# Context attentions of a small perceiver: transposes spread between products, rounding of the context moved to GpSimd

## The reference

```
q = xn @ Wq                      # 16 heads (32 wide or of other widths)
k, v = y @ Wk, y @ Wv            # y: the 1601 context rows of a batch, 128 wide
a = softmax(q k^T * scale)       # per batch and head: 64 x 1601
o = a v
```

## Time and profile before

| | |
|---|---|
| median of 3 runs | 2290.49 us (2285.55 to 2293.77) |
| the profiled execution | 2297.82 us |
| its span | 2296.0 us, 41893 instructions |
| TensorE busy | 2042.5 us, 89% |
| TensorE weight loads busy | 1749.3 us, 76% |
| VectorE busy | 1379.2 us, 60% |
| ScalarE busy | 1124.4 us, 49% |
| GpSimd busy | 512.6 us, 22% |
| granted TensorE clock, mean | 0.93 |

### The profile page before, as it was taken

One profiled execution on the slowest core, in us unless ns is written; L12 is line 12 of the kernel. 1 busy time (PEld: TensorE's weight loads), 2 busy tenths in 40 slices (PEclk: granted clock), 3 DMA queues, 4 the chain that ended last, 5 costly groups with the idle time before them and its releaser, 6 DMA issues. The chain is left out here.

```text
span 2296.0 us, 41893 instructions
## 1 busy us (share of the span) xinstructions
PE 2042.5 (89%) x14948; PEld 1749.3 (76%) x14948; DVE 1379.2 (60%) x2704; ACT 1124.4 (49%) x2256; POOL 512.6 (22%) x412
## 2 busy tenths in 40 slices
PE   4776999999886998489899999987979999999898
PEld 1654999999655885277699999956859999997577
DVE  6463777777445443831677777724447777776366
ACT  2243666666423432321566666613436666664254
POOL 2323222221011330200322222002332222220034
PEclk9687999999987998789999999977999999999799
DMA  5153010010041213432100100001221001000022
GB/s 211 25 233 128 31 45 31 29 44 0 26 156 57 79 53 136 188 139 83 45 30 31 45 29 29 0 13 66 78 83 45 31 30 44 29 15 0 19 78 76
DMA packets 32314, 144.01 MB, mean 63 GB/s; under 512 B 3632, under 2 KB 9136, under 8 KB 28848
## 3 DMA queue, kind: packets, MB, share of 16 engines
q1 hardware_dynamic: 32176, 142.23, 17.2%
HBM read 125.59 MB, written 13.90 MB: 61 GB/s over the span
## 5 line engine op out<-in xcount | busy, mean ns | idle before, releaser
L1037 ACT ACTIVATE pTh<-ps 128x512 fp32r<-128x512 f32 (+1 forms) x768 | 353.9, 519 | 382.5 <-PE ps L937 380.4
L1095 DVE TENSOR_TENSOR pTl<-ps,pTh 128x512 fp32r<-128x512 f32 (+1 forms) x768 | 415.7, 582 | 129.0 <-ACT pTh L1037 128.8
L637 PE MATMUL ps<-pTh,ch 128*128 128x256 f32 (+1 forms) x1248 | 383.5, 307 | 2.3 <-DVE pTl L1095 2.2
L638 PE MATMUL ps<-pTl,ch 128*128 128x256 f32 (+1 forms) x1248 | 348.4, 279 | 0.0
L639 PE MATMUL ps<-pTh,cl 128*128 128x256 f32 (+1 forms) x1248 | 348.0, 279 | 0.0
L637 PE MATMUL ps<-cTh,qh 128*128 128x512 f32 (+2 forms) x768 | 276.9, 361 | 15.2 <-POOL ql L891 8.0
L639 PE MATMUL ps<-cTh,ql 128*128 128x512 f32 (+2 forms) x768 | 269.6, 351 | 0.0
L638 PE MATMUL ps<-cTl,qh 128*128 128x512 f32 (+2 forms) x768 | 268.8, 350 | 0.0
L1082 DVE TENSOR_REDUCE top<-ps 128x1 f32<-128x802 f32 x192 | 189.2, 986 | 110.7 <-PE ps L639 110.7
L637 PEld LDWEIGHTS ps<-pTh,ch 128*128 128x128 f32 (+1 forms) x1248 | 235.1, 188 | 15.8 <-DVE pTl L1095 12.1
L638 PEld LDWEIGHTS ps<-pTl,ch 128*128 128x128 f32 (+1 forms) x1248 | 235.7, 189 | 0.0
(11 more groups left out here) (351 smaller groups left out, 3585.9 us busy)
## 6 DMA issues: line engine op xcount, KB each, us to landing
w<-l1f_w_in SPq DMA_DIRECT2D x16, 1024.0 KB, 8.0
raw<-ctxT_in SPq DMA_DIRECT2D x16, 801.0 KB, 4.3
raw<-ctx_in SPq DMA_DIRECT2D x14, 832.0 KB, 4.4
wg<-l0f_guide_in SPq DMA_DIRECT2D x10, 704.0 KB, 5.1
z<-ctx_in SPq DMA_DIRECT2D x8, 832.0 KB, 12.9
z<-z SPq DMA_DIRECT2D x8, 832.0 KB, 10.6
keys<-ctx_in SPq DMA_DIRECT2D x8, 832.0 KB, 11.2
zT<-zT SPq DMA_DIRECT2D x8, 801.0 KB, 14.0
```

The costliest lines, as they stand in the source:

```text
L637: pe.matmul(out, high, moving_high, start=start, stop=False)
L638: pe.matmul(out, high, moving_low, start=False, stop=False)
L1037: nc.scalar.activation(pTh[0:w, PARTS[g][0]:PARTS[g][0] + n, slot, :], ps[0:w, turned_bank[slot][g], 0:n * P].rearrange("p (k r) -> p k r" ...
L1095: dve.tensor_tensor(pTl[0:w, at, slot, :], ps[0:w, turned_bank[slot][g], 0:n * P].rearrange("p (k r) -> p k r", r=P), pTh[0:w, at, slot, : ...
```

## The change

Four edits in `cross_attention`:
- TensorE: `turn` issues one transpose. `scores` and `values` (now of one chunk) call a function after each product, which may issue one. Eight transposes of slot 1 stand between the score products of the first unit, five between the products of value chunks 0 to 2, and the thirteen of slot 0 in value chunks 5 to 12. The second unit's scores come behind value chunk 4, not 7.
- VectorE: the maximum of the first half is a function of its own and comes ahead of `low(0, v-1)`.
- ScalarE: `keep(2)` of slot 1 moves behind the exponentials of unit v; the second half of the exponential of unit v+1 moves behind `keep(2)` and `keep(3)` of slot 0. `high` is gone.
- GpSimd: `split` waits for `raw`, copies the leading part and subtracts, where `low` only subtracted.

```
@@ gpsimd
-                        def low(n, dst, high):
-
+                        def split(n, dst, high):
+
+                            pool.wait_ge(raw_landed, 16 * (n + 1))
+                            pool.sem_inc(raw_seen, 1)
+                            pool.tensor_copy(high, raw[:, 0:dst.shape[1]]).then_inc(high_ready, 1)
                             pool.wait_ge(high_ready, n + 1)
...
@@ tensor, scores
+                                cols = score_cols[n]
+                                pe.matmul(flat[:, cols], qh[:, k, at], cTh[:, i, cols], start=True, stop=False)
+                                beside(3 * n)
+                                pe.matmul(flat[:, cols], qh[:, k, at], cTl[:, i, cols], start=False, stop=False)
+                                beside(3 * n + 1)
+                                last = pe.matmul(flat[:, cols], ql[:, k, at], cTh[:, i, cols], start=False, stop=True)
                                 if n == 1:
                                     last.then_inc(scores_half, 1)
-                            last.then_inc(scores_ready, 1)
...
+                                if n == 3:
+                                    last.then_inc(scores_ready, 1)
+                                beside(3 * n + 2)
...
@@ tensor, body
-                                pe.wait_ge(probs_half, v)
-                                turn_second(0, v - 1)
-                                scores(u, step, first)
-                                turn_second(1, v - 1)
-                                turn_second(2, v - 1)
-                                values(0, c - 1, i, first and u == 2, new_batch)
-                                turn_second(3, v - 1)
-                                values(1, c - 1, i)
-                                scores(u + 1, step, first)
-                                turn_first(0, v)
-                                turn_first(1, v)
-                                values(2, c - 1, i)
-                                turn_first(2, v)
-                                values(3, c - 1, i)
-                                turn_first(3, v)
+
+                                def second_with_scores(n):
+                                    if 1 <= n < 5:
+                                        turn(0, n - 1, v - 1, 1)
+                                    elif n >= 8:
+                                        turn(1, n - 8, v - 1, 1)
+
+                                def second_with_values(n):
+                                    if n < 8 and n % 2 == 0:
+                                        turn(2, n // 2, v - 1, 1)
+                                    elif n == 8:
+                                        turn(3, 0, v - 1, 1)
+
+                                def first_with_values(n):
+                                    if 15 <= n < 19:
+                                        turn(0, n - 15, v, 0)
+                                    elif 19 <= n < 23:
+                                        turn(1, n - 19, v, 0)
+                                    elif 25 <= n < 33 and n % 2:
+                                        turn(2, (n - 25) // 2, v, 0)
+                                    elif n == 36:
+                                        turn(3, 0, v, 0)
+
+                                scores(u, step, first, second_with_scores)
+                                values(0, c - 1, i, second_with_values, first and u == 2, new_batch)
+                                for chunk in range(1, 4):
+                                    values(chunk, c - 1, i, second_with_values)
+                                values(4, c - 1, i)
+                                scores(u + 1, step, first, alone)
+                                for chunk in range(5, KCH):
+                                    values(chunk, c - 1, i, first_with_values)
...
@@ scalar, body
                                     keep(1, v - 1, 1)
-                                    keep(2, v - 1, 1)
                                 exponents(v, 0, first and u < 2, 0)
                                 exponents(v, 0, first and u < 2, 1)
                                 if before:
+                                    keep(2, v - 1, 1)
                                     keep(3, v - 1, 1)
-                                if at == 0 and not (final and i):
-                                    high(n, cTh[:, 1 - i])
-                                if at == 2 and not (final and i):
-                                    high(n + 1, ch[:, 1 - i])
                                 keep(0, v, 0, c if before else None)
                                 keep(1, v, 0, c if before else None)
                                 exponents(v + 1, 1, first and u < 2, 0)
-                                exponents(v + 1, 1, first and u < 2, 1)
                                 keep(2, v, 0, c if before else None)
                                 keep(3, v, 0, c if before else None)
...
+                                exponents(v + 1, 1, first and u < 2, 1)
...
@@ vector, body
+                                maximum_of_half(v, 0)
                                 if before:
                                     low(0, v - 1, 1)
                                 maximum(v, 0)
...
+                                maximum_of_half(v + 1, 1)
                                 maximum(v + 1, 1)
```

More of the change, by code:

```diff
@@ L914, in _, with scores @@
                     def _(pe):
-                        def scores(u, step, first):
+                        def scores(u, step, first, beside):
                             i = u // PER
@@ L933, in turn @@
[L933 to L945, removed]
-                                pe.wait_ge(low_kept, 4 * v)
-                            if g == 3:
-                                pe.wait_ge(low_kept, 4 * v + 1)
-                            turn(g, v, 0)
@@ L951, in turn_second, with turn @@
-                        def turn_second(g, v):
-                            pe.wait_ge(low_kept, 4 * v + (-2, -1, 0, 1)[g])
-                            turn(g, v, 1)
-                        def values(g, c, i, early=False, new_batch=None):
-                            if g == 0 and not early:
+                                if n == 3:
+                                    last.then_inc(scores_ready, 1)
+                                beside(3 * n + 2)
+                        def turn(g, k, v, slot, first=False):
+                            if k == 0 and slot:
+                                pe.wait_ge(low_kept, 4 * v + (-2, -1, 0, 1)[g])
+                            if k == 0 and not slot and g != 2 and (g == 3 or not first):
+                                pe.wait_ge(low_kept, 4 * v + (-1, 0, None, 1)[g])
+                            chunk = PARTS[g][k]
+                            w = keys_in(chunk)
+                            last = pe.transpose(ps[0:w, turned_bank[slot][g], k * P:(k + 1) * P],
+                                                probs[slot][:, chunk * P:chunk * P + w], ident[:])
+                            if chunk == PARTS[g][-1]:
+                                last.then_inc(turned_ready, 1)
@@ L959, in values @@
+                        def values(chunk, c, i, beside=None, early=False, new_batch=None):
+                            g = chunk // 4
+                            if chunk == 0 and not early:
                                 pe.wait_ge(value_kept, c)
@@ L979, in body @@
                                 if first and u == 0:
-                                    scores(u, step, first)
-                                    scores(u + 1, step, first)
+                                    scores(u, step, first, alone)
+                                    scores(u + 1, step, first, alone)
                                     for g in range(4):
-                                        turn_first(g, v, True)
+                                        for k in range(len(PARTS[g])):
+                                            turn(g, k, v, 0, True)
```

67 lines of the change are left out of this document (32 added, 35 removed).

## The result

The changed kernel is slower: 2334.47 us, median of 4 runs (2333.11 to 2336.07), against 2292.13 (4 runs) for the kernel before. The ratio is 1.0188, with a 95% interval of 1.0162 to 1.0214, so +42 us. The forecast was 2323.5, +33. Run again later, among the experiments, the same changed kernel took 2324.95 us (5 runs) against 2292.22: ratio 1.0155 (1.0131 to 1.0178), +33. Why the two differ is the first thing to settle, since the forecast was made on the attentions.

A forecast was written before the change was run, and what follows sets the result against it. TensorE's own instruction stream was taken as the bound. Couples +29.8 us and attention ends +3.1 gave +33, carried over to the shown median of 2290.49: 2323.5 us, range 2287 to 2342.

The forecast's parts named there:

- Transposes one by one: On TensorE, a single transpose costs 0.110 us between score products, 0.115 between value products; nothing is saved.
- Rival C: Dearer transitions on TensorE: a single transpose costs 0.136 us, +82 us, 2372 us in all; chance 7%.
- rival A: Weight loads hide on TensorE: a transpose costs 0.058 us, -60 us in the couples, 2233 us; chance 8%.
- Matching orders: TensorE waits 0.40 us at value chunk 0 for VectorE's late `low(0)`; couple 12.32 against 12.00, +29.8 us over 93.
- The second chain: Exponential ahead of second scores: ready 5.67, wanted 5.70 us; without the first wait it would hold TensorE 0.3.
- The end of each attention: TensorE waits 1.28 us for the exponential before its last transposes, 0.24 before; +3.1 us over three attentions.
- Leading parts on GpSimd: ScalarE loses 42 copies of 1.54 us, GpSimd takes them: gain 0, cost 0; 32 us as upper bound.
- The sum: Couples 29.8 us plus attention ends 3.1 us: +33 us on the whole kernel, 2323.5 us.

The follow-up runs named there:

- experiment 4: Changed kernel with the four transposes of part 2 (slot 1) ahead of value chunk 0, not among chunks 0 to 2: 2323.97 us, ratio 1.0124.
- experiment 6: Kernel before with part 1 turned behind the first unit's third score block and `low(1)` between its two reductions: 2288.54 us, ratio 0.9986.
- experiment 3: Changed kernel with `low(0, v-1)` put back ahead of the first unit's half maximum on VectorE: 2371.31 us, ratio 1.0338.
- experiment 5: Changed kernel with the second half of the second unit's exponential back ahead of `keep(2)` and `keep(3)` on ScalarE: 2321.79 us, ratio 1.0129.
- experiment 1: Kernel before with only the leading parts copied by GpSimd instead of ScalarE: 2290.16 us, ratio 0.9985.
- experiment 10: Kernel before with the edits of experiment 9 and the leading parts copied by GpSimd: 2276.59 us, ratio 0.9930.
- experiment 2: Changed kernel with each part's transposes issued together at the place of its last one: 2323.66 us, ratio 1.0131.
- experiment 9: Kernel before with `low(1)` between the reductions and part 1 turned behind the third score block's second pass: 2274.47 us, ratio 0.9916.
- experiment 8: The changed kernel run again with no edit: 2324.95 us, 5 runs.

## Why the prediction was right

Step by step, in its own order.

- *Transposes one by one.* Predicted 0.110 and 0.115, measured 0.11 and 0.115. Grouping them again gave 5 us. Rival C (0.136) and rival A (0.058) are both out. The rule of the Trainium skill, "TensorE: Matmul & The Clock Gate", section "Part 2: What happens when you issue a matmul", that weight loads are pulled ahead of running matmuls, holds here for one load behind an instruction; a second one is not hidden, as the 0.11 for a transpose that stands behind 0.233 of a product shows.
- *Matching orders.* The points of the second couple in the fences above, from its start at 1989.41 (predicted, then measured): first reduction 1.74, 1.75; `low(0)` 2.64, 2.66; load of chunk 0 3.38, 3.40; its wait 0.40, 0.38; second scores 5.82, 5.82 (of the couple before); couple 12.34 by the sum and 12.32 taken, 12.30 to 12.33. This is the term that makes the change slow.
- *The second chain.* Predicted ready at 5.67, wanted at 5.70. In the couple that starts at 1977.09, ScalarE's exponential is done at 1982.53 + 0.19, which is 5.63, so the load could go off at about 5.69, with the 0.06 that the prediction adds for the signal:

```profile
1981.70 0.93 ACT L1046 ACTIVATE normed<-ps,ntop 128x802 f32<-128x802 f32 x1 [0.71 <-DVE ntop L1100]
1982.53 0.19 ACT L1046 ACTIVATION_READ_ACCUMULATOR normed<-ps,ntop  x1
```

  That it would hold TensorE "nearly as long" without the first wait is what experiment 4 shows, with one correction: only 0.20 of it is this chain's, where the prediction had 0.3; the other 0.18 is held by `low(1)` at chunk 4, a third chain that the prediction did not have (it said only that this one is in time). It cost nothing in the forecast, since all three stand behind the same late VectorE. It did cost me the expectation of experiment 6 and the place of the wait in experiment 3.
- *The end of each attention.* Predicted a wait of 1.28, measured 1.28; undone in experiment 5 for 3 us.
- *Leading parts on GpSimd.* Predicted 0, measured 0 in experiment 1 (within 0.3%) and in experiment 10. GpSimd's copy takes 1.53 and its subtraction follows:

```profile
1986.70 1.53 POOL L880 CAST cTh<-raw 128x1602 fp32r<-128x1602 f32 x1
1988.30 3.63 POOL L882 TENSOR_TENSOR cTl<-raw,cTh 128x1602 fp32r<-128x1602 f32 x1
```

  ScalarE's busy time fell by 62 us in experiment 1 and by 30 in the changed kernel. Two copies `pTh` that follow each other overlap in the records; a pair of the kernel before counts 1.09 together:

```profile
1911.23 1.09 ACT L1037 ACTIVATE pTh<-ps 128x512 fp32r<-128x512 f32 x2 [1.71 <-PE ps L937]
```

  A single one of the changed kernel counts 0.60:

```profile
1992.70 0.60 ACT L1057 ACTIVATE pTh<-ps 128x512 fp32r<-128x512 f32 x1 [1.18 <-PE ps L949]
```

  More of them stand apart in the changed kernel: the group has 353.6 us in experiment 1 and 373.7 in the changed kernel, for 768 copies in both, of 519 and 515 ns in the mean. That accounts for 20 of the 32 us. It is no work added.
- *The sum.* +32.9 in the attentions was forecast, +35 to +36 measured. Counted from start to start in the traces, it is made up in this way. 27 of the 31 couples that the forecast counted in each attention, 81 in all, are of the usual kind; their mean goes from 12.00 to 12.33, the forecast's +0.32, and gives 26.6 us. The other four of each attention (the first two, and those with which the third and the fourth step begin) give 3.5, of which 1.5 is a single one (12.04 before, 13.53 and, when run again, 13.32); what holds that one up is open. The stretch from the last couple's first score product to the last value product goes from 18.7 to 20.4, three times 1.7, so 5.1. There the forecast had 3.1 for the wait at the end and nothing for the last couple itself, and that is most of the 2 to 3 us that it was short.
- *The sum by cause* does not close as well. 20.7 us are idle time listed ahead of the chunks' loads, 5 are for issuing singly (experiment 2), and 3.3 for the ends (experiment 5): 29 of the 35. The other 6 are not assigned by any run. In the unrolled first step the usual couple gained 0.42 (11.96 to 12.38), in the loop 0.30; why they differ is open too.
- *The number.* Both medians lie in the range, and also in the narrower 2308 to 2338 that the forecast claimed for itself. That the repeat comes within 2 us of 2323.5 is in part luck: inside the attentions the loss was 2 to 3 us larger than forecast, and outside them that execution took 9 less than the profiled one of the kernel before (1108.8 against 1117.7), mostly in the stretch that the last section is about. Of the first session's 42 us, 35 are inside.

What is not shown: no edit of the changed kernel brought the time back, and the earlier place of the second scores (behind value chunk 4, not 7) was undone in no run. In the attentions, experiments 2, 4 and 5 give 5, 5 and 4 us, and experiment 3 loses 32, since several chains are late together. That the orders are the cause rests on experiment 1 (the rounding costs nothing), on experiment 2 (issuing singly costs 5), on the wait that stands in every couple, on experiments 3 and 4, where it reappears at other places and in the size forecast, and on experiment 9, where orders alone move the couple the other way. Which of the orders costs how much is not separated.

## What to carry to other kernels

Where one engine is busy nearly throughout, as TensorE here, a pass of the loop costs the sum of that engine's instructions plus its waits. Taking work off another engine did not change that sum (experiments 1 and 10), and spreading the transposes made it a little larger (experiment 2). Before moving an instruction, write down for every consumer the moment at which it is wanted and the moment at which it is ready; all those within a few tenths of each other are the bound together, and covering one only uncovers the next (experiments 3, 4 and 6). The move that pays is the one that brings the late producer forward as early as its own input allows (experiments 6 and 9: one product earlier is the difference between 3 and 13 us in the attentions).

## What the runs showed that I had not expected

The same code can differ by 10 us and more between two executions, through TensorE's clock. The stretch between the second attention and the third takes 217.1 us in the changed kernel's first profiled execution and 209.5 in its second; over all the kernels here it takes 207 to 220, while the stretch ahead of the first attention takes 203 to 206. VectorE runs the same 2704 instructions in both executions. Set side by side, they are 2.7 us apart at 1505.6 (at the end of the second attention), 11.8 at 1566.4 and 9.3 at the end of the program. The windows view (from:to, us, busy time of TensorE, its loads, VectorE, ScalarE, GpSimd, granted clock, DMA share, GB/s) of the 36 us or so behind the second attention, in the first execution:

```profile
1524.00:1560.00 36.00, 31.12 (x107) 13.92 (x107) 9.09 (x15) 6.65 (x10) 3.57 (x3) 0.62 0.00 1
```

and in the second:

```profile
1521.00:1557.00 36.00, 30.34 (x151) 18.89 (x151) 12.14 (x25) 7.70 (x14) 3.58 (x3) 0.95 0.00 1
```

The granted clock is 0.62 in one, so much of the stretch ran at the lower of the two levels (1.2 and 2.4 GHz), and 0.95 in the other, with 151 products done instead of 107. The kernel is the same, and so is what TensorE had done before (an attention, in which it was busy for 371 and 372 of 378 us). What decides it is not settled by these runs. Within each kernel the longer executions are those with the lower mean granted clock: of the changed kernel's five runs in experiment 8, the fastest took 2321.64 us at 0.938 and the slowest 2335.67 at 0.929; the four of the first session had 0.927 to 0.932. Of the 17 runs of the kernel before beside experiments 1 to 4, the fastest took 2287.53 at 0.936 and the slowest 2299.99 at 0.929. For a comparison of two kernels it means that a difference of 10 us should be looked for by stage before it is put down to an edit.
